# Delta-rule turn: whole projections between two links of the chain, key products one place earlier

## The reference

```
q = l2norm(silu(conv4(x @ Wq))) / sqrt(128)
k, v = the same of Wk (l2norm) and Wv (no norm), two keys and two values a position
for each position:
    state = state * exp(g)
    for j in (0, 1):
        u = (v_j - k_j . state) * beta_j
        state = state + outer(k_j, u)
    o = q . state
out = (rmsnorm(o) * norm_w * silu(x @ Wg)) @ Wo
```

## Time and profile before

| | |
|---|---|
| median of the runs | 4395.57 us |
| span of the profiled execution | 4401.2 us |
| PE matmul busy | 4098.5 us, 93% |
| PE weight loads busy | 3392.4 us, 77% |
| DVE busy | 3015.5 us, 69% |
| ACT busy | 2178.4 us, 49% |
| POOL busy | 1584.0 us, 36% |

### The profile page before, as it was taken

How to read it: one execution, slowest core, us unless ns; L and a number is a source line. 1 busy time by engine, 2 the same in 40 slices (tenths; PEclk the granted TensorE clock), 3 DMA queues, 4 the chain that set the end, 5 groups by cost and what they waited for, 6 DMA issues and landing times. The chain is left out here.

```text
span 4401.2 us, 105534 instructions
## 1 busy us (share of the span) xinstructions
PE 4098.5 (93%) x36303; PEld 3392.4 (77%) x36303; DVE 3015.5 (69%) x8155; ACT 2178.4 (49%) x5662; POOL 1584.0 (36%) x2836
## 2 busy tenths in 40 slices
PE   5699999999999999999999779879999999999979
PEld 5488888888878887878888668857777777777768
DVE  4577777777777777777777444356776776776655
ACT  3355555555555555555555234344444444444344
POOL 0466666666666666666666100000000000000010
PEclk9999999999999999999999689989999999999989
DMA  4333333333333333333333142121111111111021
GB/s 159 92 81 89 80 80 90 80 80 98 91 90 80 81 93 80 85 84 80 89 80 84 57 136 86 39 78 48 52 47 38 52 48 37 52 48 48 10 69 34
DMA packets 541045, 322.11 MB, mean 73 GB/s; under 512 B 249552, under 2 KB 498896, under 8 KB 538832
## 3 DMA queue, kind: packets, MB, share of 16 engines
q1 hardware_dynamic: 540496, 315.14, 25.3%
HBM read 230.96 MB, written 83.99 MB: 72 GB/s over the span
## 5 line engine op out<-in xcount | busy, mean ns | idle before, releaser
L950 DVE SCALAR_TENSOR_TENSOR g_conv<-g_r,g_taps,g_conv 128x511 f32<-128x511 f32 (+2 forms) x961 | 698.6, 741 | 135.0 <-ACT g_conv L833 126.5
L1997 ACT ACTIVATE a_pr<-a_pr,a_low 128x128 f32<-128x128 f32 (+3 forms) x512 | 286.5, 560 | 392.0 <-DVE a_low L2142 376.0
L837 ACT ACTIVATE g_us<-g_chn 128x128 f32<-128x128 f32 x528 | 146.2, 277 | 664.0 <-PE g_chn L632 663.3
L2297 POOL TENSOR_TENSOR a_dg<-a_const,a_fl 128x384 fp32r<-128x384 f32 x32 | 26.5, 827 | 1156.4 <-DVE a_fl L2149 1156.4
L557 PE MATMUL g_r<-g_x_hi,g_w_hi 128*128 128x512 f32 x770 | 367.0, 477 | 9.4 <-issue 7.1
L2142 DVE CUSTOM_DVE_ANT_0 a_pr<-a_sc,a_bias 128x128 f32<-128x128 f32 (+3 forms) x512 | 242.3, 486 | 192.7 <-issue 173.8
L557 PE MATMUL g_r<-g_x_hi,g_w_lo 128*128 128x512 f32 x770 | 307.1, 399 | 0.0
L557 PE MATMUL g_r<-g_x_lo,g_w_hi 128*128 128x512 f32 x770 | 305.5, 397 | 0.0
L1825 PE MATMUL a_out<-a_pt,a_v 128*128 128x512 f32 (+3 forms) x1024 | 297.2, 433 | 0.9 <-DVE a_oT L2162 0.9
L833 ACT ACTIVATE g_conv<-g_r,g_taps 128x512 f32<-128x512 f32 x321 | 220.4, 687 | 135.0 <-PE g_r L557 123.4
L1151 POOL TENSOR_TENSOR g_prod<-g_small 64x14 f32<-64x14 f32 (+6 forms) x896 | 228.5, 255 | 158.7 <-DMA g_small<-lower_d 93.4
(11 more groups left out here) (358 smaller groups left out, 11974.7 us busy)
## 6 DMA issues: line engine op xcount, KB each, us to landing
g_w_raw<-w_heads SPq DMA_DIRECT2D x66, 768.0 KB, 4.9
lower_d<-g_L SPq DMA_DIRECT2D x64, 512.0 KB, 3.3
g_T<-low_d SPq DMA_DIRECT2D x64, 512.0 KB, 5.0
g_U<-upp_d SPq DMA_DIRECT2D x64, 512.0 KB, 6.3
a_w<-w_groups SPq DMA_DIRECT2D x32, 640.0 KB, 4.6
oT_d<-g_oT SPq DMA_DIRECT2D x67, 256.0 KB, 6.3
f_oT<-oT_d SPq DMA_DIRECT2D x8, 2048.0 KB, 9.4
a_wo<-wo_b SPq DMA_DIRECT2D x32, 512.0 KB, 5.4
```

What stands on the lines that cost most here:

```text
L950: ins = V.scalar_tensor_tensor(out=y[:, k:L], in0=x[:, 0:L - k], scalar=tap, in1=y[:, k:L], op0=ALU.mult, op1=ALU.add)
L1997: A(pr[g % 2][:, i, 0:width(i)], pr[g % 2][:, i, 0:width(i)], ACT.Exp, scale=-1.0, bias=low[g % 2][:, i:i + 1], accum_out=tot[g % 2][:, i: ...
```

## The change

Only the order of PE's list in turn is changed. No instruction is added or removed, no wait's value is changed, and the lists of the other engines stay.

```diff
                 chain_u(u, par, 0)
                 if own:
                     pe.wait_ge(s["d_bv"], 2 * u + 1)
-                    project(u, par, V0, (0,))
+                    project(u, par, V0)
                 chain_s(u, q, 0, made)
-                if own:
-                    project(u, par, V0, (1,))
                 chain_ks(u, q, 1)
                 if own:
                     pe.wait_ge(s["d_bv"], 2 * u + 2)
-                    project(u, par, QB, (0,))
+                    project(u, par, QB)
                 chain_u(u, par, 1)
-                if own:
-                    project(u, par, QB, (1,))
-                chain_s(u, q, 1, made)
                 if own:
                     pe.wait_ge(s["d_silu"], 5 * u + 4)
                     transposes(ktr_b[0], lambda c: keys(kT[q])[:, c, :], HC, s["d_ktr"])
+                chain_s(u, q, 1, made)
+                if own:
+                    transposes(ktr_b[1], lambda c: keys(kT[q])[:, HC + c, :], HC, s["d_ktr"])
                 chain_ks(u, q, 2)
                 if own:
-                    transposes(ktr_b[1], lambda c: keys(kT[q])[:, HC + c, :], HC, s["d_ktr"])
+                    gram(0)
                 chain_u(u, par, 2)
                 if own:
-                    gram(0)
+                    gram(1)
                 chain_s(u, q, 2, made)
                 if own:
-                    gram(1)
+                    pe.wait_ge(s["d_conv"], 5 * u + 4)
+                    project(u, par, V1)
                 chain_ks(u, q, 3)
-                if own:
-                    pe.wait_ge(s["d_conv"], 5 * u + 4)
-                    project(u, par, V1, (0,))
                 chain_u(u, par, 3)
                 if own:
-                    project(u, par, V1, (1,))
+                    pe.wait_ge(s["d_conv"], 5 * u + 5)
+                    project(u, par, GB)
                 chain_s(u, q, 3, made)
-                if own:
-                    pe.wait_ge(s["d_conv"], 5 * u + 5)
-                    project(u, par, GB, (0,))
-                chain_ks(u, q, 4)
-                if own:
-                    project(u, par, GB, (1,))
-                chain_u(u, par, 4)
                 if own:
                     pe.wait_ge(s["d_silu"], 5 * u + 6)
                     pe.wait_ge(s["d_kend"], 2 * u + 3)
                     pe.wait_ge(s["d_ksq"], 2 * u + 1)
                     read_out(0)
+                chain_ks(u, q, 4)
+                if own:
+                    read_out(1).then_inc(s["d_kq"], 1)
+                chain_u(u, par, 4)
                 chain_s(u, q, 4, made)
-                if own:
-                    read_out(1).then_inc(s["d_kq"], 1)
                 if inverse:
                     have_inverse(u, own)
                 chain_ks(u, q, 5)
```

More of the change, by code:

```diff
@@ L719, in turn @@
                     read_out(0)
-                chain_s(u, q, 4, made)
+                chain_ks(u, q, 4)
                 if own:
                     read_out(1).then_inc(s["d_kq"], 1)
+                chain_u(u, par, 4)
+                chain_s(u, q, 4, made)
                 if inverse:
```

## The result

The changed kernel takes 4587.94 us, the median of 4 runs (4577.38 to 4591.17), against 4394.38 us for the kernel before, the median of 4 runs (4390.56 to 4404.54): a ratio of 1.0437, 95% interval 1.0421 to 1.0452. It is slower by 194 us. The forecast was 4571 us, with a range of 4500 to 4610.

The account below looks back on a forecast made before the run. PE's in-order stream was taken as the bound. Lost cover of 3.0 us over 64 turns: span 4401.2 + 192 - 17 = 4576, less 5.6 from span to median, 4571 us; range 4500 to 4610.

Parts of the forecast that it names:

- QB whole: Undivided QB projection behind u(1): key transposes wait for silu(K1), 1.11 us of empty PE; chain_s(1) 1.29 us late.
- V1 whole: Undivided V1 projection ahead of ks(3): nothing left between ks(3) and u(3); lateness grows from 1.01 to 1.61 us.
- GB whole: Undivided GB projection behind u(3) waits for QB's last tap on DVE; chain_s(3) is 2.05 us late.
- read-out up a place: Nothing left between u(4) and chain_s(4), nor independent work before ks(5): lateness 2.62, then 2.90, with restart 3.0 us a turn.
- Transposes and Gram moved up: Around ks(2) and u(2): u(2)'s earlier 0.17 us wait disappears, lateness falls from 1.29 to 1.12 us.
- V0 whole: Undivided V0 projection before chain_s(0), nothing between it and ks(1): 0.07 us late, between zero and 0.2.
- What is given back: DVE's lower waits for dm, 17.2 us in 21 turns, end: minus 17 us, possibly nothing or 40.
- POOL's ring: POOL's substitution and the next chain_s(0) both move 3.7 us, so the 3 us of slack between them stay.
- One: Rival: silu(K1) does not hold the transposes; about 1.7 us a turn from the other holes, 4489 us; chance 0.07.
- Three: Rival: new pauses lower PE's granted clock for some 3 us of each turn, 4667 us; chance 0.04.
- Four: Rival: nothing changes, since the 19% without weight loads lets PE catch up after holes, 4396 us; chance 0.04.
- Two: Rival: POOL's ring sets the turn, PE's holes fall into waiting time and earlier work helps, about 4365 us; chance 0.05.

## Why the prediction was right

The mechanism was right. PE's stream was the bound, no work was removed, and the new order takes cover from five places. "QB whole": the dearest step, the transposes' wait for silu(K1), came 63 times in 63; shortening it from ACT's side gave 44 us and from PE's side 32, where 45 and 29 were expected. "V1 whole", "GB whole" and "read-out up a place": each wait stands in the trace with the releaser named, and in the turn shown the distances between the links differ from the walk's by 0.1 us at most. "Transposes and Gram moved up": u(2), which waited before, follows without a wait. "V0 whole: between zero and 0.2": zero, as far as 0.17% can tell.

The sizes. The walk gave 192 us and the give-back took off 17, which leaves 175; the trace shows 64 x 2.89 = 185. The 10 us between them are the next step's. The rest of the way from 4571 to the measured 4588 is no part of the mechanism: the forecast took off 5.6 us because the profiled execution before lay above its runs' median, and the profiled execution after lies 4.1 below its own (4583.8 against 4587.94). That the sum comes out so well is in part luck: the last 0.11 us a turn of the walk, for the restart of ks(5), hardly shows (0.93 us from ks(5) to u(5) in the changed kernel, 0.89 before).

"What is given back." This step had half of it. The wait for g_dm did go, as predicted, all 17 us. But the prediction itself moves POOL's substitution back by 3.7 us, more than the 3.0 by which the turn grows, so g_qg and g_dmt run deeper into the time at which DVE has g_qden to do: in the median turn g_dmt starts 1.03 us ahead of u(0) before the change and 0.72 ahead after it, and g_qden starts 0.21 ahead in both. With the 64 executions of g_qden 29.1 us too long before and 38.8 after, some 10 us are lost anew. "POOL's ring ... its 3 us of slack stay" was true and missed this: I asked who waits for POOL's result, not what POOL's running does to DVE.

The rivals. One (silu does not hold the transposes) is excluded by three runs. Three (the clock) is excluded by the granted clock of 0.99 after: up to the last turn the clock was at 0.50 for 23.8 us in both kernels. The 63 waits of 0.91 us did not bring it down, while longer waits in other versions did, as above. Four (19% of headroom) is excluded by the result itself: the holes in PE's list lengthened the turn by about their sum, so a weight-load time of 81% left no room. The Trainium skill (Perfetto Trace Analysis, "Identifying the Most-Contended Engine") rightly warns of matmul busy time, but here the distance from start to start was the reading that held. Two (POOL's ring) was wrong as a forecast and right in its object. The ring does not decide while PE is slower, but an order better than the kernel before meets it at once, in single late turns and not as a floor under all of them.

## What to carry to other kernels

When an in-order engine is the bound and its list alternates links of a serial chain with independent work, count for each gap between two links what stands in it against the answer's delay (here 0.6 us beside the link's own product), and never put a piece ahead of a link if its own input is made by the engine that must first answer that link. Whole blocks do not buy anything there; small pieces spread to fit do.
When such an order has been made tighter and gains less than its holes, look for the second ring, for two engines shutting each other out, and at the granted clock of the longest turns, before giving the idea up: three edits that gave 15 us less, 15 us less and 114 us more gave 51 us less together.

## What the runs showed of the hardware

A DVE operation from SBUF to SBUF on 128x4 numbers (0.15 us alone) does not run beside POOL's elementwise operations: it ended 0.02 to 0.03 us after POOL's, with 0.78 us for one and 2.04 us for another that met two of them. DVE's taps, which read PSUM and one tile of SBUF, kept 0.74 us beside POOL. Nor is it the size that matters: two DVE operations on 128x8 numbers of SBUF, one behind the other (changed kernel, ns min/median/max), differ in the same way.

```profile
L1026 DVE TENSOR_SCALAR g_ss<-g_ss x64: 158/218/1018, 176.9 to 2610.8; 128x8 f32<-128x8 f32 x64
...
L1027 DVE RECIPROCAL g_rk<-g_ss x64: 202/203/205, 177.0 to 2610.9; 128x8 f32<-128x8 f32 x64
```

The reciprocal kept its 0.20 us in all 64 executions, 19 of which lay wholly within an operation of POOL. The tensor_scalar was stretched up to 1.02 us. The Trainium skill (SBUF — State Buffer, "Who interferes with whom") says so: VectorE and GpSimd take one pair of ports in turns, the loser blocked for the other's whole instruction, and only for VectorE operations in certain modes, which a tensor_scalar can enter, or with two SBUF inputs. The runs agree. g_qden and g_ss are tensor_scalar operations with one input, so by that page only the modes are left for them; no run here shows the mode itself.

A matmul for which PE had to wait cost 0.11 us beyond the wait (1.03 us from ks(1) to u(1) against 0.92 from u(1) to chain_s(1), with the same work between); chain_s(4) to ks(5) shows it again in the changed kernel, 0.93 where 0.83 is the answer's delay alone.
